# LoRA B and LoRA-down B as pairs of 64-row products, with B loaded once per tile

## What is computed

```python
def lora_add(base, inp, A, B):
    Ab = A[layer_idx][lora_indices]
    Bb = B[layer_idx][lora_indices]
    t = jnp.einsum('bri,bni->bnr', Ab, inp)
    return base + jnp.einsum('bor,bnr->bno', Bb, t) * SCALE
gate = lora_add(jnp.einsum('bnh,fh->bnf', x, W_gate), x, A_gate, B_gate)
up = lora_add(jnp.einsum('bnh,fh->bnf', x, W_up), x, A_up, B_up)
act = jax.nn.silu(gate) * up
down = lora_add(jnp.einsum('bnf,hf->bnh', act, W_down), act, A_down, B_down)
```

## Time and profile before

| what | value |
| --- | --- |
| median of 3 runs | 1098.61 us (1097.95 to 1099.84) |
| profiled execution, its own time | 1099.33 us |
| its span, first to last instruction | 1097.5 us |
| mean granted TensorE clock | 0.988 |
| PE busy | 1045.0 us, 95% |
| POOL, ACT, DVE busy | 487.3, 405.1, 267.2 us |
| DMA engines, mean share in the tiles | about 36% |

### The profile page before, as it was taken

One profiled execution on the slowest core, in us unless ns is written; L12 is line 12 of the kernel. 1 busy time (PEld: TensorE's weight loads), 2 busy tenths in 40 slices (PEclk: granted clock), 3 DMA queues, 4 the chain that ended last, 5 costly groups with the idle time before them and its releaser, 6 DMA issues.

```text
span 1097.5 us, 18681 instructions
## 1 busy us (share of the span) xinstructions
PE 1045.0 (95%) x6048; PEld 918.6 (84%) x6048; DVE 267.2 (24%) x519; ACT 405.1 (37%) x627; POOL 487.3 (44%) x301
## 2 busy tenths in 40 slices
PE   3399699999999999999999999999999999999997
PEld 3266488988988999888989988999888989989996
DVE  8433212222222122222212222222222212222222
ACT  7002143443344334434443344334434443344331
POOL 0702454544554445445444544445454544544441
PEclk9699899999999999999999999999999999999999
DMA  9799342433333342424243333434242433333320
GB/s 343 266 311 340 108 133 68 136 97 110 102 104 108 98 124 89 130 60 142 81 118 105 101 106 96 124 96 119 82 133 68 134 96 108 100 105 109 109 66 20
DMA packets 100979, 135.49 MB, mean 123 GB/s; under 512 B 26395, under 2 KB 59420, under 8 KB 100956
## 3 DMA queue, kind: packets, MB, share of 16 engines
q1 hardware_dynamic: 100380, 135.12, 40.4%
q10 hardware_dynamic: 576, 0.08, 0.0%
HBM read 118.11 MB, written 16.99 MB: 123 GB/s over the span
## 4 chain that ended last, share of the span: by engine, by line
PE 93%; SPq 3%; DMA 2%; issue 1%; ACT 0%; DVE 0%; DVEq 0%
PE ps L928 45%; PE ps L970 26%; PE ps L938 7%; PE ps L901 6%; PE ps L959 4%; PE ps L912 2%; SPq L201 1%; PE ps L918 1%; DMA tm_d<-wms 1%; SPq L269 1%; PE ps L983 1%; PE ps L982 1%; PE ps L946 1%; SPq L206 1%; DMA braw<-in_tb 0%
## 5 line engine op out<-in xcount | busy, mean ns | idle before, releaser
L928 PE MATMUL ps<-wg_hi,x_hi 128*128 128x512 f32 (+2 forms) x768 | 296.5, 386 | 1.6 <-DVE x_lo L781 1.6
L928 PE MATMUL ps<-wg_lo,x_hi 128*128 128x512 f32 (+2 forms) x768 | 290.7, 378 | 0.0
L928 PE MATMUL ps<-wg_hi,x_lo 128*128 128x512 f32 (+2 forms) x768 | 290.6, 378 | 0.0
L448 POOL TENSOR_TENSOR bst<-braw,bst 128x1024 fp32r<-128x1024 f32 (+1 forms) x96 | 213.1, 2219 | 116.1 <-ACT bst L547 116.1
L563 ACT ACTIVATE at_hi<-ps 128x512 fp32r<-128x512 f32 (+1 forms) x96 | 54.0, 562 | 303.5 <-PE ps L959 301.9
L928 PEld LDWEIGHTS ps<-wg_hi,x_lo 128*128 128x128 f32 x768 | 144.5, 188 | 25.5
L928 PEld LDWEIGHTS ps<-wg_hi,x_hi 128*128 128x128 f32 x768 | 144.8, 189 | 23.9 <-issue 2.0
L928 PEld LDWEIGHTS ps<-wg_lo,x_hi 128*128 128x128 f32 x768 | 145.0, 189 | 21.6
L970 PE MATMUL ps<-wd_hi,at_hi 128*128 128x288 f32 (+1 forms) x704 | 155.3, 302 | 1.4 <-DVE at_lo L804 1.4
L970 PE MATMUL ps<-wd_hi,at_lo 128*128 128x288 f32 (+1 forms) x704 | 150.9, 296 | 0.0
L970 PE MATMUL ps<-wd_lo,at_hi 128*128 128x288 f32 (+1 forms) x704 | 150.3, 295 | 0.0
(11 more groups left out here) (138 smaller groups left out, 1075.5 us busy)
## 6 DMA issues: line engine op xcount, KB each, us to landing
braw<-in_tb SPq DMA_DIRECT2D x256, 128.0 KB, 2.7
braw<-in_tb SPq DMA_DIRECT2D x128, 96.0 KB, 2.4
adraw<-in_tad SPq DMA_DIRECT2D x128, 88.0 KB, 1.9
tr<-kpad SPq DMA_DIRECT2D x16, 512.0 KB, 6.4
xb<-in_x SPq DMA_DIRECT2D x32, 256.0 KB, 2.9
agraw<-in_ta SPq DMA_DIRECT2D x128, 64.0 KB, 2.0
bdraw<-in_tbd SPq DMA_DIRECT2D x128, 64.0 KB, 2.2
x1p<-yo SPq DMA_DIRECT2D x16, 512.0 KB, 4.1
```

Of the source, the lines that this page charges most:

```text
L448: sub(v, b_from(p, q), v.bitcast(F32), ALU.subtract).then_inc(s["blo"], 1)
L928: last = mm(bank[:, 0:n], x3s[a][:, k, :], wgs[b][:, k, o:o + n], start=(k == 0 and a + b == 0), stop=False, skip_group_check=True)
```

## The change

Gate's B stands in rows 0 to 63 and up's B in rows 64 to 127, each rank once. The hi and lo parts get buffers of their own (b_hi, b_lo, and bd_hi, bd_lo for the down adapter). lora_b makes the three passes with products of 64 rows, gate and up in turn: gate's reads rows 0 to 63 and writes gate's bank, up's reads rows 64 to 127 and writes up's bank. lora_b_down does so with the left and the right part of the result. B of a whole tile is loaded at once (load_b), a tile ahead, in 8 DMAs; B-down takes 8 DMAs too. The first B-down load moves from the convolution to the start of the tiles. Masked t has 128 columns instead of 256, so t_turn is one turn instead of two.

```diff
@@ -129,10 +128,9 @@
-        brs = [sb("braw0", [P, 4 * 2 * P])]
-        bdraw = sb("bdraw", [P, T])
+        brs = [sb("braw0", [P, FP])]
...
-        bst = sb("bst", [P, 2, 4 * 2 * P], F32R)
-        bdst = sb("bdst", [P, T], F32R)
+        bst = [sb("b_hi", [P, 2, 4 * P], F32R), sb("b_lo", [P, 2, 4 * P], F32R)]
+        bdraw = sb("bdraw", [P, DH])
+        bdst = [sb("bd_hi", [P, DH], F32R), sb("bd_lo", [P, DH], F32R)]
...
+        def rank_rows(tile, u, b):
+
+            return tile[u * NAD + b:(u + 1) * NAD:GB, :]
...
-            def load_b(t, e, p, q, free=None):
+            def load_b(e, p, free=None):
                 if free is not None:
                     sp.wait_ge(s["blo"], free)
                     sp.sem_inc(s["bfree"], 1)
-                o, w = PAIRS[q][0] * 2 * P, (PAIRS[q][1] - PAIRS[q][0]) * 2 * P
                 for b in range(GB):
-                    rows = tb[e[b], :, o:o + w].rearrange("a k w -> (a k) w")
-                    sp.dma_start(brs[(p + q) % 2][b * 2 * RANK:(b + 1) * 2 * RANK, 0:w],
-                                 rows.unsqueeze(1).to_broadcast([RANK, 2, w])).then_inc(s[f"b{(p + q) % 2}"], 16)
+                    rows = tb[e[b]].rearrange("a r (j u f) -> (a r) j u f", u=2, f=P)
+                    for u in range(2):
+                        sp.dma_start(rank_rows(brs[p], u, b).rearrange("r (j f) -> r j f", f=P),
+                                     rows[:, :, u, :]).then_inc(s[f"b{p}"], 16)
...
-            def tile_io(t, p, here, there, mixes, first=False, last=False):
+            def tile_io(t, p, there, mixes, first=False, last=False):
                 if not last:
                     load_x(t + 1)
-                load_b(t, here, p, 2, t * 3 + 1)
-                if not last:
+                    load_b(there, 1 - p, None if first else t * 3)
                     load_ag(t + 1, there)
                     load_ad(t + 1, there)
                     load_wbd(t if not first else None, mixes, 1 - p)
-                    load_b(t + 1, there, 1 - p, 0, t * 3 + 2)
                 if not first:
                     store_out(t - 1)
                 if not last:
-                    load_b(t + 1, there, 1 - p, 1, t * 3 + 3)
                     load_bd(t + 1, there)
...
-            load_b(0, here, 0, 0)
+            load_b(here, 0)
             load_ad(0, here, True)
-            load_bd(0, here, True)
...
+            load_bd(0, entries(SP, 0, 0, NA, 0, GB), True)
             block_io(0, first=True)
...
             def lora_b(t, p, q):
                 pe.wait_ge(s["blo"], t * 3 + q + 1)
                 w = FW[q]
-                n = (PAIRS[q][1] - PAIRS[q][0]) * P
-                for u in range(2):
-                    for a in range(2):
-                        last = mm(gub[2 * ((p + q) % 2) + u][:, 0:w], ts2[a][:, u, :],
-                                  bst[:, (p + q) % 2, u * n:u * n + w], start=False, stop=(a == 1),
-                                  skip_group_check=True)
+                for a, b in PASSES:
+                    for u in range(2):
+                        rows = slice(u * NAD, (u + 1) * NAD)
+                        last = mm(gub[2 * ((p + q) % 2) + u][:, 0:w], ts2[a][rows, :], bst[b][rows, (p + q) % 2, 0:w],
+                                  start=False, stop=(a == 1), skip_group_check=True)
                 last.then_inc(s["gu"], 1)
 
             def t_turn(t):
                 pe.wait_ge(s["tm"], t + 1)
-                for u in range(2):
-                    last = nc.tensor.transpose(misc[:, u * P:(u + 1) * P], tm[:, u, :], ident)
-                last.then_inc(s["tmt"], 1)
+                nc.tensor.transpose(misc[:, 0:P], tm[:], ident).then_inc(s["tmt"], 1)
...
-                for a in range(2):
-                    mm(left, tds[a][:], bdst[:, 0:cut], start=False, stop=(a == 1), skip_group_check=True)
-                    last = mm(right, tds[a][:], bdst[:, cut:T], start=False, stop=(a == 1), skip_group_check=True)
+                for a, b in PASSES:
+                    mm(left, tds[a][0:NAD, :], bdst[b][0:NAD, 0:cut], start=False, stop=(a == 1), skip_group_check=True)
+                    last = mm(right, tds[a][NAD:P, :], bdst[b][NAD:P, cut - (T - DH):DH], start=False, stop=(a == 1),
+                              skip_group_check=True)
                 last.then_inc(s["accd"], 1)
```

More of the change, by code:

```diff
@@ L169, in cond_resid_kernel @@
         ats = [sb("at_hi", [P, T], F32R), sb("at_lo", [P, T], F32R)]
[L170 to L171 removed]
+        tm = sb("tm", [P, P])
+        ts2 = [sb("t_hi", [P, P], F32R), sb("t_lo", [P, P], F32R)]
         tdm = sb("tdm", [P, P])
@@ L245, in ad_from, with b_view @@
             return adraw[:].rearrange("p (b r j) -> p j b r", b=GB, j=FT)
-        def b_view(p, q):
-            n = PAIRS[q][1] - PAIRS[q][0]
-            return bst[:, (p + q) % 2, 0:n * 2 * P].rearrange("p (u j f) -> p j u f", u=2, f=P)
+        def b_view(tile, p, q):
+            return tile[:, (p + q) % 2, 0:(PAIRS[q][1] - PAIRS[q][0]) * P]
         def b_from(p, q):
-            n = PAIRS[q][1] - PAIRS[q][0]
-            return brs[(p + q) % 2][:, 0:n * 2 * P].rearrange("p (j u f) -> p j u f", u=2, f=P)
+            return brs[p][:, PAIRS[q][0] * P:PAIRS[q][1] * P]
+        def rank_rows(tile, u, b):
+            return tile[u * NAD + b:(u + 1) * NAD:GB, :]
         block = ctx.enter_context(nc.Block())
@@ L325, in load_bd @@
                     rows = tbd[e[b]].rearrange("a k w -> (a k) w")
-                    sp.dma_start(bdraw[b * 2 * RANK:(b + 1) * 2 * RANK, :],
-                                 rows.unsqueeze(1).to_broadcast([RANK, 2, T])).then_inc(s["bd"], 16)
+                    for h in range(2):
+                        sp.dma_start(rank_rows(bdraw, h, b), rows[:, h * (T - DH):h * (T - DH) + DH]).then_inc(s["bd"], 16)
             def store_out(t):
@@ L353, in block_io @@
                 after = None if last else entries(SP, i + 1, 1, NCOND, 0, GB)
-                if first:
-                    load_b(0, here[0:GB], 0, 1)
-                tile_io(i * 2, 0, here[0:GB], here[GB:], mixes, first=first)
-                tile_io(i * 2 + 1, 1, here[GB:], there, after, last=last)
+                tile_io(i * 2, 0, here[GB:], mixes, first=first)
+                tile_io(i * 2 + 1, 1, there, after, last=last)
             sp.wait_ge(s["kout"], 32)
@@ L542, in b_high @@
             def b_high(t, p, q, free=None):
[L543 to L544 removed]
+                act.wait_ge(s[f"b{p}"], (t - p) * 16 * GB + 32 * GB)
                 if free is not None:
                     act.wait_ge(s["gu"], free)
[L547 removed]
+                copy(b_view(bst[0], p, q), b_from(p, q), ACT.Copy).then_inc(s["bhi"], 1)
             def bd_high(t, first=False):
[L550 removed]
+                act.wait_ge(s["bd"], (t + 1) * 32 * GB)
                 if not first:
                     act.wait_ge(s["accd"], t)
[L553 removed]
+                copy(bdst[0][:], bdraw[:], ACT.Copy).then_inc(s["bdhi"], 1)
             def silu(t, p, q):
@@ L566, in t_high @@
                 act.wait_ge(s["tmt"], t + 1)
-                copy(ts2[0][:].rearrange("p u n -> p (u n)"), misc[:, 0:2 * P], ACT.Copy).then_inc(s["thi2"], 1)
+                copy(ts2[0][:], misc[:, 0:P], ACT.Copy).then_inc(s["thi2"], 1)
             def td_high(t):
```

33 lines of the change are left out of this document (11 added, 22 removed).

## The result

The change makes the kernel slower: 1116.95 us (1115.63 to 1117.80), against 1099.22 us of the kernel before measured beside it, ratio 1.0161 [1.0148, 1.0173]. I had forecast 1086.3 us, in a range of 1073 to 1112. The profiled execution took 1115.63 us, with a span of 1113.8. First the page of the changed kernel, for the earlier trace rows, and the same stretch of the tiles as in the earlier trace rows.

A forecast was written before the change was run, and what follows sets the result against it. TensorE's own instruction stream was taken to bound the tiles. Savings of 25.9 us, less 9.6 for changes of height and 4.0 at the start, gave -12.3 from 1099.33: 1087.0, or 1086.3 for the median; range 1073 to 1112.

The forecast's parts named there:

- Pairs side by side: In lora_b and lora_b_down, a pair costs one product; with one turn less, 0.81 us a tile saved; chance 0.66.
- The rival of serial halves: In lora_b and lora_b_down, one half runs after the other: 44 us more in the tiles, 1147 in all; chance 0.10.
- Partial overlap: Rival in the pairs: a pair costs 1.3 products; 1099 us without a cost of changes, 1108 with it; chance 0.09.
- Entering and leaving the halves: TensorE's six changes a tile between full height and halves, 192 in all: 0.05 us each, 9.6 us.
- the turns: Trace rows around TensorE's turns, 0.11 us each, with no time left over for a change: lower bound of nothing.
- the upper bound: At each change of height the whole overlap between products is lost: 0.16 us each, 30.7 us in all.
- The draining rival: At the six changes of height a tile the array empties, 0.16 us each: +8.8 us, 1107; chance 0.15.
- The start: Later loads in SyncE's queue move tile 1's mix 3.5 us back; 4.0 us cost in all, bounds nothing to 7.5.
- The load of B in the convolution: Replaces B and B-down loads of about the same bytes in shorter pieces: costed at nothing, at most 1 us.
- The queue's own delay: SyncE's queue at the start: x late by 4.5 us, A, A-down and wbd 7.5 us late.
- the new wait of 3.2 us for b_low: Tile 0, lora_b for q = 1: TensorE could start at 143.0, but GpSimd's b_low is ready at 146.2.
- From tile 1 on: SyncE's loads of A and wbd move by 3.0 us a tile, landing some 2 us to spare: costs nothing.

The follow-up runs named there:

- same_half: Changed kernel with both members of each pair on rows 0 to 63, so they must follow one another: 1189.22 us, ratio 1.0815.
- six_full: Changed kernel with every LoRA B and LoRA-down B product over all 128 rows instead of 64, same number and width of products: 1151.40 us, ratio 1.0471.
- rows96: Changed kernel with every LoRA B and LoRA-down B product over rows 0 to 95 instead of 64 rows: 1152.27 us, ratio 1.0482.
- split_down: Changed kernel with lora_b_down no longer next to lora_b of q = 1, two more changes of height a tile: 1131.32 us, ratio 1.0289.

## Why the prediction was wrong

**Pairs side by side: right.** Members start together, pairs follow each other like single products (0.23 to 0.24), and without the pairs a tile takes 2.22 us more (same_half). So the saving of 0.81 us a tile is there. The rival of serial halves gave six starts at even steps and 1147; that is what six_full, without pairs, looks like (1151.40). Partial overlap is out too. The Trainium skill's 3.07 times for four tiles (TensorE: Matmul & The Clock Gate, Measured speedup vs the span model), on which that rival leaned, doesn't carry over to two tiles here: the trace has one product's time for two.

**Entering and leaving the halves: the step that failed.** I chose 0.05 us a crossing between 0 and 0.16; it is 0.19 to 0.20. This term alone turns the sign: 192 x 0.197 = 37.8 us instead of 9.6, against 25.9 saved. Two errors lie in it. I leaned to the turns because they were "the only change of use that the trace has". But a turn has all 128 rows; rows96 shows that even fewer rows cost nothing as long as the array isn't halved. The turns were no evidence on halving, though they were the nearest rows. And the upper bound was too low. I counted the lost overlap of two products but not that the next weights no longer load ahead. That price stood in the trace of the kernel before, where lora_b's first product in tile 0 meets an empty array:

```profile
136.30 0.19 PEld L938 LDWEIGHTS ps<-bst,t_hi 128*128 128x128 f32 x1 [1.17 <-DVE t_lo L793]
...
136.30 0.43 PE L938 MATMUL ps<-bst,t_hi 128*128 128x352 f32 x1 [0.93 <-DVE t_lo L793]
136.57 0.33 PE L938 MATMUL ps<-bst,t_lo 128*128 128x352 f32 x1
```

Weights and product start together, and the next product follows after 0.27, not 0.16: 0.11 for weights that weren't loaded ahead. With the 0.16 of overlap an upper bound of 0.27 would have been due; 192 of these are 52 us, and with the start of 4.0 and the 25.9 saved the bound would have stood near 1128.5. The measured crossing is a smaller gap (0.09) plus the same 0.10. This split is read from the starts; no run takes the two parts apart.

**The draining rival: right in kind, undersized.** It gave 0.16 a crossing and 1107, with a chance of 0.15. It named the signs (a gap of 0.1 or more on both sides, a tile of 30.1; it is 0.09 and 0.10 on each side, 30.32) and the point from which it decides, 0.114. The Trainium skill's rule spoke for it; I gave more weight to the turns.

**The start: the number right, partly by luck.** The forecast was 3.5 us at mix of tile 1 and 4.0 in all; it is 3.96 at mix. That ScalarE and a_turn are held up by the late load of A, and that mix ends last, came as forecast: a_turn waits 1.4 us, mix 0.8 for wbd. But the parts are others. The load of B in the convolution, "at nothing, at most 1 us", may have brought up to 1.9 us. The queue's own delay was smaller: wbd is issued 7.52 us later than before, the 7.5 of the forecast, but 1.92 of that is the later end of the convolution, so the queue added 5.6; for x it added 3.8 instead of 4.5. And the new wait of 3.2 us for b_low didn't come. lora_b for q = 1 of tile 0 starts at 145.71, 0.32 behind the product ahead, which is a crossing and no wait. b_low was done at 145.48 instead of 146.2, and TensorE, forecast for 143.0, was itself late by the convolution and by the lower clock.

**From tile 1 on** the prediction was that loads of A and wbd cost nothing. No wait of TensorE for them appears in the tiles behind tile 1; right.

The sum with the measured terms: 3.95 ahead of tile 1's chunk (the excursions of tile 0 are in it), and for the 31 tiles' worth behind it -0.81 x 31 + 0.197 x 6 x 31 = +11.5. Together 15.5, against 16.3 in the span.

## What to carry to other kernels

In this kernel a change of how the array is divided has a price of its own, paid when entering and when leaving, and it is paid per excursion, not per product: count the crossings first, and set them against what an excursion saves. Here three pairs of 512 columns save 0.23 us and cost 0.38, so by these numbers pairs pay only when several such groups stand together, and here even joining them came to no more than even. What decides is measured by a pair of runs that differ in the crossings alone, as six_full and same_half do. When a bound is built from "the overlap is lost", add what else the overlap hides, above all weights loaded ahead, and look for the place where the trace has an emptied engine, not for one that merely looks like a change.

## What the runs showed of the hardware

A change between products of 128 rows and products of 64 rows costs TensorE 0.19 to 0.20 us (1.15 us for six in the timeline; 37.8 us for 192 between same_half and six_full), also when both products of each pair lie in the same half; the two more of split_down came to 0.23 each. Two products of 64 rows on different halves take the time of one (0.24 us from pair to pair at 512 columns, and 2.22 us a tile less than same_half). Products of 96 rows among those of 128 cost nothing that can be measured (1152.27 against 1151.40 us). What I hadn't expected is the part of the weight loads: at such changes the load doesn't run ahead of its product (190 waits, 0.30 us on average); between products of full height that wait for no data it does, in six_full and rows96 everywhere in the tiles but once. Starting TensorE's next product with its weights not yet in costs 0.10 to 0.11 us (0.33 instead of 0.23 behind 613.81; 0.27 instead of 0.16 behind 136.30 in the kernel before).
